# Four PSUM banks for scores and two for the max pass, in place of three and three

## The reference

```python
q = (x @ q_w + q_b).reshape(Bx, Tx, NH, HD).transpose(0, 2, 1, 3)
...
att = jnp.einsum('bhqd,bhkd->bhqk', q, k) * (1.0 / np.sqrt(HD))
att = att + build_alibi_bias(NH, Tx)[None]
att = jnp.where(causal[None, None], att, -jnp.inf)
att = jax.nn.softmax(att, axis=-1)
y = jnp.einsum('bhqk,bhkd->bhqd', att, v)
...
x = _layernorm(x + _L0_attn_ref(...), axis=-1)
x = _layernorm(x + _L0_ffn_ref(...), axis=-1)
```

## Time and profile before

| | before |
|---|---|
| median of 3 runs | 1083.16 us (1081.72 to 1083.65) |
| the profiled execution, its own time | 1081.94 us |
| its span, first to last instruction | 1080.2 us |
| PE busy | 1007.4 us, 93% |
| DVE busy | 735.1 us, 68% |
| ACT busy | 769.7 us, 71% |
| POOL busy | 650.1 us, 60% |

### The profile page before, as it was taken

One profiled execution on the slowest core, in us unless ns is written; L12 is line 12 of the kernel. 1 busy time (PEld: TensorE's weight loads), 2 busy tenths in 40 slices (PEclk: granted clock), 3 DMA queues, 4 the chain that ended last, 5 costly groups with the idle time before them and its releaser, 6 DMA issues. The chain is left out here.

```text
span 1080.2 us, 27381 instructions
## 1 busy us (share of the span) xinstructions
PE 1007.4 (93%) x8726; PEld 673.4 (62%) x8726; DVE 735.1 (68%) x2012; ACT 769.7 (71%) x1706; POOL 650.1 (60%) x1164
## 2 busy tenths in 40 slices
PE   2999999999999998999999869989999999999992
PEld 0444454445444543544454338889999999999882
DVE  2898888888888888888888126844333335666595
ACT  1168888888888876888888854467777777788553
POOL 1035565546554554888888953567777775666442
PEclk9789999999999998999999989999999999999996
DMA  5332333323332331344332234022333223444343
GB/s 148 83 98 69 91 82 103 88 81 84 102 91 80 90 96 56 103 119 112 87 99 53 72 114 179 24 73 84 84 84 84 81 73 98 124 129 134 90 138 95
DMA packets 123388, 102.02 MB, mean 94 GB/s; under 512 B 18880, under 2 KB 113862, under 8 KB 122594
## 3 DMA queue, kind: packets, MB, share of 16 engines
q1 hardware_dynamic: 113362, 78.18, 26.8%
q0 software_dynamic: 8640, 16.87, 4.8%
q10 hardware_dynamic: 1248, 5.21, 1.3%
HBM read 39.51 MB, written 35.66 MB: 70 GB/s over the span
## 5 line engine op out<-in xcount | busy, mean ns | idle before, releaser
L740 ACT ACTIVATE probs<-scores 128x512 f32<-128x512 f32 x640 | 354.3, 599 | 55.2 <-PE scores L637 53.8
L811 POOL TENSOR_SCALAR_AFFINE_SELECT probs<-probs 128x256 f32<-128x256 f32 (+1 forms) x640 | 222.5, 362 | 155.2 <-ACT probs L740 145.3
L637 PE MATMUL scores<-qstack,kstack 64*128 64x512 bf16 (+3 forms) x1024 | 225.2, 302 | 4.3 <-ACT probs L740 3.7
L1246 DVE TENSOR_TENSOR e_hid<-e_gate,e_up_ps 128x352 f32<-128x352 f32 (+2 forms) x190 | 106.5, 561 | 179.1 <-ACT e_gate L1521 159.7
L653 PE MATMUL pv<-probs,vaug 128*32 128x512 f32 (+3 forms) x2048 | 193.2, 450 | 1.1 <-POOL probs L811 1.1
L942 DVE CUSTOM_DVE_ANT_0 summed<-maxed,last_mask 128x512 bf16<-128x512 f32 x256 | 166.5, 682 | 26.1 <-PE maxed L609 23.9
L1604 POOL DMA_INDIRECT y_tokens<-e_raw,e_row_i x142 | 140.3, 988 | 65.9 <-issue 30.1
L949 DVE TENSOR_REDUCE maxB<-maxed 128x4 f32<-128x512 f32 x256 | 164.9, 679 | 16.2 <-PE maxed L620 14.5
L637 PEld LDWEIGHTS scores<-qstack,kstack 64*128 64x128 bf16 x1024 | 65.8, 94 | 160.2 <-ACT probs L740 99.4
L614 PE MATMUL maxed<-kstack,qstack 64*128 64x128 bf16 (+2 forms) x768 | 144.4, 283 | 8.0 <-DVE maxB L949 7.6
L1521 ACT ACTIVATE e_gate<-e_gate_ps 128x352 f32<-128x352 f32 (+2 forms) x190 | 94.4, 497 | 76.3 <-PE e_gate_ps L1418 47.6
(11 more groups left out here) (194 smaller groups left out, 1709.5 us busy)
## 6 DMA issues: line engine op xcount, KB each, us to landing
qstack<-parts SPq DMA_DIRECT2D x96, 128.0 KB
kstack<-parts SPq DMA_DIRECT2D x96, 128.0 KB
x_sorted<-zeros SPq DMA_DIRECT2D x16, 580.5 KB, 5.2
e_xs<-x_sorted SPq DMA_DIRECT2D x142, 64.5 KB
e_raw<-y_tokens SPq DMA_DIRECT2D x64, 128.0 KB
xin<-in_x SPq DMA_DIRECT2D x16, 256.0 KB, 3.4
e_group_in<-x1T_all SPq DMA_DIRECT2D x16, 256.0 KB, 2.9
out<-e_raw SPq DMA_DIRECT2D x64, 64.0 KB
```

What stands on the lines that cost most here:

```text
L637: last = pe.matmul(scores[st.at(0, SEQ_UNITS, n) % SB][:, col:col + width], ks[rows, slot, kt * P:(kt + 1) * P], q[rows, slot, kt * P:T], ...
L740: act.activation(probs[g % 2][:, u * T:(u + 1) * T], scores[st.at(0, SEQ_UNITS, UNITS * g + u) % SB][:], ACT.Exp).then_inc(S["exp_done"], 1)
L811: pool.affine_select(out=view, in_=view, compare_op=ALU.is_ge, fill=0.0, base=0, pattern=pattern, channel_multiplier=-1).then_inc(S["maske ...
L1246: dve.tensor_tensor(hid[step % len(hid)][rows, 0:cols], gate[step % 2][rows, 0:cols], up_ps[step % 2][rows, 0:cols], ALU.mult).then_inc(S[ ...
```

## The change

One line. The bank of scores is one more, the bank of the max pass one fewer; the eight banks are still all in use. Both waits shown above and the choice of the bank (`% SB`, `% MB`, in TensorE's, ScalarE's and VectorE's code) follow from it. The sequence of instructions is the same on all five engines; only the values that the waits name, and the banks' addresses, differ.

```diff
-SB, MB = 3, 3
+SB, MB = 4, 2
```

## The result

| | before | after |
|---|---|---|
| median | 1083.41 us (1081.72 to 1084.50, 4 runs) | 1167.51 us (1166.94 to 1171.22, 4 runs) |
| ratio | 1 | 1.0785 (95% interval 1.0759 to 1.0811) |
| the profiled execution, its own time | 1081.94 us | 1171.22 us |
| its span | 1080.2 us | 1169.5 us |

The change makes the kernel 84.1 us slower, 7.8%. 1156 was forecast; the time lies inside the range, 11.5 us above its middle.

The account below looks back on a forecast made before the run. PE's own sequence, with its waits for max banks inside, was taken as the bound; 58.8 + 12 + 3.5 - 1 = 73.3 us on 1081.94 gave 1155.2, and 1.2 more for the median 1156 us, range 1140 to 1172.

Parts of the forecast that it names:

- What bounds the kernel: Whole attention: PE's own sequence, with its waits for max banks inside, sets the step of 35.91 us.
- The regular steps: Twelve attention steps: delays at max banks that wait for take n-2 add 4.89 us each, 58.8 in all.
- one distance that held take 1: From job "m" to take 2, 1.20 us kept from before; part of max 37 to max 4, +0.37 a step.
- The clock in the regular steps: PEclk in the regular attention steps, claimed to stay at 1.00.
- The rival on the clock: Waits around max 37 to 39 lower PE's clock, 3 us more a step, 15 x 3 = 45: 1201; chance 0.06.
- The special steps: First step with units, routing step, last max pass: bounded by 2 and 5 us, 4 taken each, 12 in all.
- The start: While the pipeline fills, some 40 max banks with slower turns: between 1.6 and 12 us, 3.5 taken.
- The score bank: Fourth score bank, mostly in the last sequence: saves between 0 and 3.7 us, 1 taken.
- the delays add: Regular steps; the rival said VectorE's slack catches up, leaving 1.75 us a step, 26 in all, 1109; chance 0.06.
- the score banks weren't the bound: L637's idle; the rival took it as real bank waits, a fourth bank winning 16 us in all, 1067; chance 0.03.

Follow-up runs that it names:

- half takes: Takes read every second column of their bank: 1115.61 us against the changed kernel (four score, two max banks), 1070.68 us against the kernel before (three and three).
- the trace with the filling: Changed kernel plus matmuls nobody reads, 24 before the first max bank and two per unit place in the second filling step: 1168.02 us, ratio 1.0782; profiled execution 1162.20.

## Right and wrong, point by point

**What bounds the kernel:** right. PE's own sequence with the waits for max banks inside sets the step. The half takes show that VectorE is on the path through the length of one take, and not through the sum of its work.

**The regular steps:** right, 56.6 of 58.8 us. The 0.33 a step too much came from one distance that held take 1; over twelve steps that is 4.0 us, and the 3.4 of the clock hid most of it.

**The clock in the regular steps:** PEclk was to stay at 1.00. In three of the twelve it didn't. This is PE's row of the timeline of after, and one of the table of stretches, behind the close turns of max 37 to 39 in the step that begins at 272.78:

```profile
305.00 1.76 PE L653 MATMUL pv<-probs,vaug 128*32 128x512 f32 x8
```

```profile
306.00:307.00 1.00, 1.00 (x6) 0.13 (x4) 0.36 (x2) 0.19 (x1) 0.27 (x1) 0.50 0.00 0
```

The `pv` takes 1.76 where it took 1.07, and the clock is back at 309. Such a step is 1.1 to 1.2 us longer (41.61 against 40.47), some 3.4 us in the run. The rival on the clock so came at the place that it named, but in a quarter of the steps and at a third of its price, where it had put 3 us in each of 15. The Trainium skill, "TensorE: Matmul & The Clock Gate", section on psum-queue depth-cycling, has the mechanism (a clock that goes to and fro where PE stands still briefly between groups as it cycles through its banks); this trace agrees with it in three of twelve steps, and disagrees in the other nine, which have the same gaps and kept 1.00. In the start it shows something else: a level that stayed low past 80 us.

**The special steps:** 18.7 in place of 12. Routing (3.6) and last max pass (5.5) stand near the 4 that I took, though the last is above my bound of 5. The first step with units cost 9.6. Its first part still ran at the lower clock (L543 at 80.72), and the trace with the filling, which has no added matmuls in this step, shows what that is worth. From the first unit to the next step's it took there, at the upper level:

```profile
68.17:102.59 34.42, 31.35 (x295) 13.42 (x292) 28.30 (x63) 25.40 (x50) 15.67 (x40) 1.00 0.29 78
```

That is 4.0 above before (30.45, from 59.70 to 90.15), as I took; after needs 40.08 (71.17 to 111.25), so the other 5.7 go with the clock. This I had not seen: I treated it as a regular step.

**The start:** the term that was mis-sized. I took 3.5 of 1.6 to 12 "because projections and transposes lie between them"; it was 10.7. My reason for a value near the low end failed. The low end is the turn at the upper level, 0.64 in place of 0.60 a bank; but after ran the filling at the lower level, as before itself did from 42 to 62 us, and there the turn measured 0.80 a bank, 8 us over the second filling step. My upper bound had that mechanism, at 0.91 a bank. The value should have been taken near it, and the next step's with it: L543 is still slow at 80.72 in after, where before had it fast from 62.63 on.

**The score bank:** -1 was forecast. PE's idle at L637 fell by 3, the time didn't, and the kernel without the fourth bank is the same within its interval.

**The rivals that fell:** the delays add (the table of places); the score banks weren't the bound (with two max banks a regular step is 40.47 with three score banks as with four).

Of the forecast's error against the profiled execution, 16 us, the three starting steps are 12.8 (20.3 less 7.5). The rest is small and of both signs.

## What to carry to other kernels

Where one engine fills banks and another empties them in strict turn, count one turn (filled, taken, filled again) and lay it, with one bank fewer, at each place along the producer's own order; delays at places where the emptying engine had itself been waiting add up, whatever its busy share says. Here a bank was worth more to the pass with the longer turn, and the wait with the largest sum in the list pointed to the other. Price the stages that fill the pipeline by themselves, with a turn at the lower clock where the trace shows that level in them.

## What the runs showed of the hardware that was not expected

PE's lower level outlasted what I thought of as the start: matmuls of 512 columns took 2.07 us until beyond 80 us of the span where PE had waits in each few us, and 1.12 from 42 us on in a kernel with the same banks whose PE had not stood still for the 10 us before. The clock column can contradict that, 1.00 beside matmuls of double length. In regular steps with the same instructions the clock fell for some 3 us in three steps and not in nine. And with PE busy throughout the lower level held in one profile for nearly 60 us. The runs don't show what decides it.
